# Keys turned by VectorE in blocks of 32 and by transfers through memory, and projected ahead of the queries

## The reference, cut to what matters

```python
# x: 2 sequences of 2048 tokens of 256; H = 16 heads, S = 64, LV = 12 levels
Q, K = x @ Wq.T, x @ Wk.T                     # per head 64 wide
V = x @ Wv.T                                  # per head 16 wide
Lam = softplus(Lp * (x @ Wdl.T))              # 12 level weights per head and token
g = -exp(A_log) * softplus(x @ Wdt.T + dt_bias)
cg = cumsum(g)
scores[t, s] = Q[t] . K[s] / 8
Wmat = scores * exp(cg[t] - cg[s]) * Lam[t, level(t, s)]   # s <= t; level = bit length of s XOR t
o = (Wmat @ V) @ Wout.T + x                   # then layernorm with gain and bias
x = layernorm(x + o)
# then a gated recurrent cell over the 2 sequences (3 gates, 256 wide), outputs through tanh,
# added to x, and a last layernorm
```

## Time and profile before

| | us |
|---|---|
| median of 3 runs | 671.96 |
| lowest, highest | 671.46, 676.09 |
| profiled execution | 675.62 |
| its span | 674.0 |

### The profile page before, as it was taken

The page is one execution under the profiler, slowest core; times in us unless marked ns, Lnnn a source line. Parts: engine busy times, 40 slices in busy tenths (PEclk is TensorE's granted clock), DMA queues, the critical chain, the costliest instruction groups (busy, mean ns, idle before and its releaser), DMA issues.

```text
span 674.0 us, 22147 instructions
## 1 busy us (share of the span) xinstructions
PE 656.2 (97%) x9114; PEld 594.3 (88%) x9114; DVE 486.4 (72%) x1100; ACT 336.9 (50%) x755; POOL 354.1 (53%) x475
## 2 busy tenths in 40 slices
PE   9989999999999999999999999999998999999994
PEld 7889999999999999899999999999987788888894
DVE  3864887779787978676887879787986656655556
ACT  5555454444545454555454445545552343555555
POOL 1806555646464646556554636474883335343425
PEclk9999999999999999999999999999997999999998
DMA  9123130414131222203140313122336403140002
GB/s 304 51 58 64 45 89 28 92 31 88 41 77 54 66 65 67 69 27 87 31 93 28 89 30 88 36 67 74 92 81 126 68 9 62 52 82 31 33 33 93
DMA packets 91987, 45.47 MB, mean 67 GB/s; under 512 B 39664, under 2 KB 90480, under 8 KB 91888
## 3 DMA queue, kind: packets, MB, share of 16 engines
q1 hardware_dynamic: 91888, 44.06, 26.6%
HBM read 34.60 MB, written 9.44 MB: 65 GB/s over the span
## 4 chain that ended last, share of the span: by engine, by line
PE 85%; DVE 6%; ACT 2%; POOL 2%; issue 2%; SPq 1%; DMA 0%; DVEq 0%; POOLq 0%
PE bank L436 64%; PE bank L460 5%; PE bank L439 4%; PE bank L527 4%; PE bank L492 4%; PE bank L556 4%; DVE t L1027 1%; ACT t L790 1%; SPq L347 1%; DVE t L1030 1%; ACT E L790 1%; SPq L370 1%; POOL t L1414 1%; DMA yT<-xscr 0%; POOL yL L1414 0%
## 5 line engine op out<-in xcount | busy, mean ns | idle before, releaser
L436 PE MATMUL bank<-xH,wH 128*128 128x256 f32 x480 | 144.4, 301 | 1.2 <-ACT KT L790 0.9
L436 PE MATMUL bank<-xL,wH 128*128 128x256 f32 x480 | 135.0, 281 | 0.0
L436 PE MATMUL bank<-xH,wL 128*128 128x256 f32 x480 | 134.5, 280 | 0.0
L1027 DVE TENSOR_TENSOR W<-bank,E 128x512 f32<-128x512 f32 x128 | 82.1, 685 | 23.9 <-PE bank L436 23.6
L436 PEld LDWEIGHTS bank<-xH,wH 128*128 128x128 f32 x480 | 90.4, 188 | 7.8 <-issue 7.3
L436 PEld LDWEIGHTS bank<-xL,wH 128*128 128x128 f32 x480 | 90.5, 189 | 0.4
L436 PEld LDWEIGHTS bank<-xH,wL 128*128 128x128 f32 x480 | 90.5, 188 | 0.0
L790 ACT ACTIVATE E<-bank 128x512 f32<-128x512 f32 x128 | 66.1, 602 | 46.8 <-PE bank L460 46.8
L790 ACT ACTIVATE QT<-bank 128x512 f32<-128x512 f32 x64 | 38.2, 597 | 98.5 <-PE bank L436 98.5
L436 PE MATMUL bank<-QT,KT 64*128 64x128 f32 x1024 | 66.3, 280 | 0.0
L436 PEld LDWEIGHTS bank<-QT,KT 64*128 64x128 f32 x1024 | 60.2, 189 | 4.8 <-issue 0.8
(11 more groups left out here) (151 smaller groups left out, 1650.5 us busy)
## 6 DMA issues: line engine op xcount, KB each, us to landing
cB<-scr SPq DMA_DIRECT2D x240, 64.0 KB, 3.0
xt<-in_xT SPq DMA_DIRECT2D x16, 256.0 KB, 2.8
xs<-in_x SPq DMA_DIRECT2D x16, 256.0 KB, 3.2
xscr<-tx SPq DMA_DIRECT2D x32, 128.0 KB, 2.8
yT<-xscr SPq DMA_DIRECT2D x64, 64.0 KB, 2.5
out<-xs SPq DMA_DIRECT2D x16, 256.0 KB, 2.1
xt<-in_wffn SPq DMA_DIRECT2D x8, 256.0 KB, 3.0
QT<-in_wqk SPq DMA_DIRECT2D x4, 256.0 KB, 5.8
```

Source lines behind the costliest of these rows:

```text
L436: return e.matmul(o, a, b, start=start, stop=stop)
L1027: return e.tensor_tensor(o, a, b, op)
```

## The change

TensorE's transposes of keys and ScalarE's copies of them are gone. VectorE turns each quarter of a pair's KT (128x512) in blocks of 32x32 into a buffer kx (`turn_keys`; for pair 0 into W), and SyncE stores it in memory, kscr (`store_keys`). `load_keys` reads a chunk's keys back into Kt with four transfers that put the blocks in their places, in runs of 32 numbers. The state matmuls wait for these. In a pair from the second on, jobs 0, 1, 4, 5 now make K and jobs 2, 3, 6, 7 make Q (`part`). `load_coefs` is split, so that key transfers stand between its parts. x1 is gone (the sum is written in place in xs), tx is one buffer instead of two, and the columns of the second part's weights are ordered to follow the new order of jobs.

```diff
--- before.py
+++ after.py
-SPLIT = [0, 4, 1, 5, 2, 6, 3, 7]
+SPLIT = [4, 5, 0, 1, 6, 7, 2, 3]
...
+def part(sg, j):
+
+    if sg == 0:
+        return j % 2 == 0, j - j % 2
+
+    return j % 4 >= 2, 4 * (j // 4) + 2 * (j % 2)
+
+
+def copied(sg, q):
+
+    return next(j for j in range(8) if part(sg, j) == (False, 2 * q)) + 1
+
+
+def key_jobs(s):
+
+    out = []
+    for d, q in ((7, 0), (5, 1), (3, 2), (2, 3)):
+        if (s + d) % 8 == 0 and 1 <= (s + d) // 8 < NSG:
+            out.append(((s + d) // 8, q))
+    return out
...
-        if s % 4 == 0 and cc < CB - 1:
-            out += [("keys", ci, 0), ("keys", ci, 1)]
...
+        kscr = nc.dram_tensor("kscr", (4 * NSG, 32, 2048), F32, kind="Internal").ap()
...
-        x1 = sb("x1", [P, 256])
-        tx = [sb(f"tx{i}", [P, 256]) for i in range(2)]
+        tx = sb("tx", [P, 256])
+        kx = sb("kx", [P, 512])
...
+            def store_keys(sg, q):
+
+                e.wait_ge(d_kx, 4 * sg + q + 1)
+                src, done = (kx[:, :], l_kx) if sg else (W[:, 4 * q:4 * q + 4, :].rearrange("p h t -> p (h t)"), l_k0)
+                e.dma_start(kscr[4 * sg:4 * sg + 4, :, 512 * q:512 * q + 512].rearrange("i t c -> (i t) c"),
+                            src).then_inc(done, 16)
+
+            def load_keys(ci):
+
+                sg, c = ci // 2, ci % 2
+                e.wait_ge(l_kx, 64 * sg) if sg else e.wait_ge(l_k0, 64)
+                if STATE[ci]:
+                    e.wait_ge(p_st, STATE[ci])
+                for j in range(4):
+                    b = 128 * c + 32 * j
+                    e.dma_start(Kt[32 * j:32 * j + 32, :].rearrange("t (q i f) -> t q i f", q=8, i=4),
+                                kscr[4 * sg:4 * sg + 4, :, :].rearrange("i t (q b) -> t q i b", q=8)[:, :, :, b:b + 32]
+                                ).then_inc(l_Kt, 16)
...
                 for sg, j in token_jobs(s):
                     if j == 5:
-                        load_coefs(sg)
-                        if sg + 2 < NSG:
-                            load_x(sg + 2)
+                        store_coefs(sg)
...
-                if s in (NG - 8, NG - 7):
-                    load_turned(0, s - NG + 8)
                 if (ci := chunk_at(s, 11)) is not None:
                     store_turned(ci)
+                for q in range(4) if s == -2 else ():
+                    store_keys(0, q)
+                for sg, q in key_jobs(s):
+                    store_keys(sg, q)
+
+                if 0 <= s < NG and s % 8 == 3 and s // 4 + 1 in STATE:
+                    load_keys(s // 4 + 1)
+                if -1 <= s < NG - 8 and s % 8 == 7:
+                    load_keys((s + 1) // 4)
+                if s == -1:
+                    load_coefs(0, 1)
+                    e.wait_ge(g_xl, 1)
+                    load_xt(3)
+                    load_x(2)
+                if s in (NG - 10, NG - 7):
+                    load_turned(0, (s - NG + 10) // 3)
+                for sg, j in token_jobs(s):
+                    if j == 5:
+                        load_coefs(sg, 0)
+                for sg, j in token_jobs(s - 1):
+                    if j == 5:
+                        load_coefs(sg, 1)
+                        if sg + 2 < NSG:
+                            load_x(sg + 2)
...
-                    for q in range(4):
-                        t = tr(MB[m][:, 128 * q:128 * q + 128], KT[b][:, 4 * n + q, 128 * c:128 * c + 128])
-                    t.then_inc(p_kt, 1)
...
+                e.wait_ge(l_Kt, 64 * (STATE[ci] + 1))
...
-                b, Q, q = sg % 2, banks[project_bank(j)], j % 2 == 0
-                m0 = j if q else 8 + j - 1
+                b, Q = sg % 2, banks[project_bank(j)]
+                q, m0 = part(sg, j)
+                m0 = m0 if q else 8 + m0
...
-                    act(Kt[:, 512 * n:512 * n + 512], MB[m][:, :], ACT.Copy).then_inc(m_free[m], 1)
...
+                if ci == 0:
+                    e.wait_ge(l_k0, 64)
...
-                e.transpose(tx[ci % 2][:, :], xs[:, ci, :]).then_inc(d_tx, 1)
+                if ci:
+                    e.wait_ge(l_tx, 16 * ci)
+                e.transpose(tx[:, :], xs[:, ci, :]).then_inc(d_tx, 1)
+
+            def turn_keys(sg, q):
+                e.wait_ge(a_qk, 8 * sg + copied(sg, q))
+                src = KT[sg % 2][:, 2 * q:2 * q + 2, :].rearrange("p m t -> p (m t)")
+                if sg == 0:
+                    o = W[:, 4 * q:4 * q + 4, :].rearrange("p h t -> p (h t)")
+                else:
+                    o = kx[:, :]
+                    if sg > 1 or q:
+                        e.wait_ge(l_kx, 16 * (4 * (sg - 1) + q))
+                e.transpose(o, src).then_inc(d_kx, 1)
...
+                if s == -2:
+
+                    for q in range(4):
+                        turn_keys(0, q)
...
+                for sg, q in key_jobs(s):
+                    turn_keys(sg, q)
...
-                    tt(x1[:, :], oo[:, :], xs[:, ci, :], ALU.add).then_inc(g_x1, 1)
+                    tt(xs[:, ci, :], oo[:, :], xs[:, ci, :], ALU.add).then_inc(g_x1, 1)
```

More of the change, by code:

```diff
@@ L29 @@
 B_END = 1200
-WF, WI, WC, UF, UI, UC, WO, UO = range(8)
+GX, GU, WO, UO = (4, 5, 0), (1, 6, 7), 2, 3
 def bc(ap, axis, n):
@@ L337, in load_coefs @@
                 e.dma_start(scr.rearrange("a l c t -> (a l) (c t)"), cT[:, :]).then_inc(l_sc, 16)
+            def load_coefs(sg, c):
                 e.wait_ge(l_sc, 16 * sg + 16)
[L339 to L348, removed]
+                ci = 2 * sg + c
+                if ci in INTER:
+                    if ci >= 2 and ci - 2 in INTER:
+                        for h in range(2):
+                            m, u = MISC["inter", ci - 2, h]
+                            e.wait_ge(m_free[m], u + 1)
+                    for a in range(8):
+                        e.dma_start(cB[c][16 * a:16 * a + 16, :, :, :].rearrange("p l u t -> p (l u) t"),
+                                    scr[a, :, c, :].partition_broadcast(16)).then_inc(l_cB[c], 16)
@@ L355, in load_turned @@
             def load_turned(blk, t):
                 c0 = 16 * t + 4 * blk
-                for i in range(2):
-                    e.wait_ge(l_tx[i], 16 * (c0 // 2 + 2))
+                e.wait_ge(l_tx, 16 * (c0 + 4))
                 if blk == 0:
@@ L391, in _ @@
             load_xt(2)
-            load_coefs(0)
-            e.wait_ge(g_xl, 1)
-            load_xt(3)
-            load_x(2)
+            store_coefs(0)
             for s in STEPS:
-                for i in [i for i in range(8) if s == (NG - 20 if i < 2 else NG - 17 + i)]:
+                for i in [i for i in range(8) if s == (NG - 20 if i < 2 else min(NG - 17 + i, NG - 10))]:
                     load_wf(i)
@@ L592, in first_project @@
             def first_project(j):
-                q = j % 2 == 0
-                Q, m0 = banks[5 * (j % 2)], j if q else 8 + j - 1
+                q, m0 = part(0, j)
+                Q, m0 = banks[5 * (j % 2)], m0 if q else 8 + m0
                 if j < 4:
@@ L646, in first_bias @@
                 e.wait_ge(a_qk, 8 * NSG)
-                e.wait_ge(g_wf, SPLIT.index(UC) + 1)
+                e.wait_ge(g_wf, max(SPLIT.index(w) for w in GU) + 1)
                 e.wait_ge(g_c0, 1)
@@ L751, in _ @@
                 if 0 <= ci < NC:
-                    if n == 0 and ci in STATE:
-                        keys(ci)
                     if n == 1:
@@ L806, in project @@
                 n = 5 * (j % 2) if sg == 0 else project_bank(j)
-                b, q = sg % 2, j % 2 == 0
-                m0 = j if q else 8 + j - 1
+                b = sg % 2
+                q, m0 = part(sg, j)
                 src = banks[n][:, :].rearrange("p (m t) -> p m t", m=2)
@@ L815, in project @@
                     e.wait_ge(p_sc, 4 * (sg - 2) + 4)
+                    e.wait_ge(d_kx, 4 * (sg - 2) + 4)
                 if q:
@@ L989, in _ @@
                     act(c0H[:, :, :], bc(c0, 2, 2), ACT.Copy).then_inc(a_c0, 1)
-                if 0 <= s < NG and s % 4 == 0 and s // 4 in STATE:
-                    keys(s // 4)
                 for sg, j in project_jobs(s):
```

56 lines of the change are left out of this document (18 added, 38 removed).

## The result

The changed kernel takes **724.44 us** (median of 4 runs, 716.97 to 727.8) against 672.10 for the kernel before in the same comparison (4 runs): ratio **1.073**, 95% interval 1.062 to 1.083. It is slower, by about 52 us, where 12 less were forecast, and it lies outside the range. The profiled execution took 727.8 us, its span is 726.0. It is the slowest of the four, and the ratio rests on the other three (716.97 to 726.99).

The account below looks back on a forecast made before the run. TensorE was taken as the bound; -25.5 (transposes) + 11.2 (Kt waits) + 1 (start) + 1 (last pair) = -12.3 us, giving 660 us against a median of 671.96; range 647 to 690 us.

Parts of the forecast that it names:

- What bounds the kernel: TensorE: busy 97% of the span, 85% of the chain of waits; an instruction removed mid-program gives its issue time back.
- The transposes, -25.5: Thirty chunks lose eight key transposes each on TensorE, at a step of 0.85 us per chunk: 25.5 us saved.
- estimate of 94 us: The skill's 390 ns per TensorE turn for 240 transposes, time about 570 us; set aside for the measured 106 ns.
- The Kt wait, +11.2: State matmuls of each pair's first chunk wait 0.8 us for Kt (bounds 0 and 2.7), 14 times: +11.2 us (0 to +38).
- Kt late: Rival: queue ahead of Kt load stretches, landing 6.2 us, wait 2.8 us per pair, about 689 us; chance of late 0.27.
- break-even of 1.7 us: The Kt wait per pair, 23.5 / 14, beyond which the change turns to a loss; over 1% at 2.2 us.
- The clock: TensorE's granted clock might drop to 0.50 behind each new wait: about 1.5 us each, 20 in all, outside the sum.
- VectorE, costed at nothing: Added turns fit VectorE's idle gaps at no cost; rival: turns and store waits pass on 10.5 us, 670 us; shared chance 0.15.
- Kt in time: Rival: Kt loads land in under 4.5 us, only a 0.2 us CT wait shows: -20.7, 651 us; chance 0.20.
- Start: Program start: first Kt lands at 44.6, where the first state would stand at 44.0: +1 us (0 to 3).
- Last pair: Chunk 30's Kt lands at 518.0, state stood at 512.85; mostly offset by the vanishing 2.62 us yL wait: +1 (0 to 6).
- The 19-fold loss: Skill's warning that a DMA copy turning by access pattern is 19 times slower than hardware transpose; judged not to apply here.

Follow-up runs that it names:

- experiment 12: Changed kernel with second cB set and xs load behind Kt loads, two kx buffers, nearly all turns cut to 32 of 512 columns: 667.41 us, ratio 0.990.
- experiment 10: Changed kernel halved: VectorE turns only odd chunks' keys, even ones transposed on TensorE; both turns moved, one behind the state update: 662.41 us, ratio 0.983.
- experiment 7: Changed kernel with second cB set and xs load behind Kt loads, one kx buffer, nearly all turns cut to 32 of 512 columns: 669.34 us, ratio 0.993.
- experiment 1: Changed kernel with a pair's second set of cB loads and its xs load moved behind the first chunk's Kt loads: 680.31 us, ratio 1.009.
- experiment 3: Changed kernel plus 20 useless matmuls before the Kt wait of even chunks 2 to 26: 707.42 us, ratio 1.050.
- experiment 4: Changed kernel with TensorE's key transposes and ScalarE's copies put back; turns, stores and loads stay, no state waits for Kt: 686.14 us, ratio 1.019.
- 5: Changed kernel with second cB set and xs load behind Kt loads, plus a second buffer for turned keys (pairs 1 to 12): 673.48 us, ratio 1.000.
- experiment 2: Changed kernel with Kt loads of the same bytes in 4096-byte runs per partition instead of 128-byte pieces: 686.26 us, ratio 1.020.
- experiment 9: Changed kernel, two kx buffers, second cB set behind Kt, first yT loads behind last Kt, turns moved to idle places, pair 14's cB behind weights: 674.30 us.
- 6: Changed kernel with second cB set and xs load behind Kt loads, two kx buffers, first eight yT loads behind the last Kt load: 674.05 us, ratio 1.000.

## Why the prediction was wrong

**What bounds the kernel**: right. TensorE is busy over 91% of the interior in every row above, and what the experiments took out of its waits and its slow clock came back in the time.

**The transposes, -25.5**: right in kind, too large. One row pair gave a step of 0.85 us; the interior of experiment 12 gives 0.70 (17.6 / 25), so 30 chunks are worth 21.1; by experiment 10 (busy TensorE 9.4 us less for 12 chunks) it is 0.78, or 23.5. In experiment 7 the first matmul comes 1.02 us behind the start of the weighing (340.60 to 341.62), as the first transpose did before (314.70 to 315.71), so there the whole 0.85 is saved. Yet a whole chunk took 13.76 us (338.46 to 352.22) against 14.38 before, only 0.62 less: elsewhere in the chunk some is lost again, 0.12 of it in the ng piece, which starts 0.98 us behind wo,yt instead of 0.86. One step was taken where a whole period should have been. The prediction's estimate of 94 us for the transposes was carried to "about 570 us"; with the other terms of the sum it gives 592, without them 578. Nothing else rests on it.

**The Kt wait, +11.2: this step failed.** Its parts: issue of the first Kt load 10.4 us after the store of keys 2, measured 11.0 in the pair above, near enough. From that issue to the state 5.3 us were taken, between bounds of 4.1 and 7.2. Measured are 6.1 to 8.3, 7.1 in the mean over the 14 pairs. The 5.3 took the *transfer* time of the yT set and left out what the *issue* takes: a Kt load of 1024 pieces holds the queue 0.98 us (3.9 for four, mean), a cB or yT load 0.53 to 0.59. Three such issues and the landing, 4.1 us in experiment 1 (the page's median, against yT's 2.5), are 7.0. I had put aside the upper bound, which was the very same number of pieces, timed in full. With 7.1 the wait is 2.6 us by the prediction's own sum; 2.4 was measured. In the list of rivals this was "Kt late", and its break-even of 1.7 us was passed. By itself it adds 22 us to the forecast, 14 waits of 2.4 us instead of 0.8, and turns the gain of 12 into a loss of 10.

**The clock, left out of the sum.** It stood in the rival as 1.5 us a wait, 20 us. It belonged to every case with a wait. In the interior TensorE was busy 413.8 us; with the same instructions at full clock in experiment 12, 391.0. So **22.8 us** of the loss is slow clock (18.8 if experiment 1, with its small waits, is the measure), 1.75 us for each of the 13 Kt waits of the interior, near the 1.5 that the rival had. The granted clock of the interior, 0.95 in its row, gives some 23 us without any comparison, and experiment 3 won 17 us back by doing more work.

**VectorE, costed at nothing**: wrong, but hidden in the changed kernel, since the waits for Kt gave VectorE time to catch up. It shows when they are gone: experiment 4 puts the price of the added work at 12.3 us with nothing gained, most of it waits for VectorE, 5 puts the store wait out of kx at 8.0 us of TensorE (named as a rival, with 3.2 us of landing against 3.65 of work before the next turn; but the store sits behind loads in the queue, and the wait for it was up to 2.6 us). The first rival, "Kt in time", with its 651 us, was therefore too good: with Kt in time the kernel takes 680, with the second buffer 673.

**The ends**. Start: +1 forecast, 2.2 measured, inside its bounds, but by luck. The first state was to wait for the late Kt; it stood at 47.23, 2.4 us later than before, with no wait in front of it, though its Kt was issued at 37.50. What came instead was a longer wait for ng, a result of VectorE, and the low clock right behind it (0.57 over 42 to 46 us). Before the change the same matmul stood at 40.38, with 0.53 us of wait; now:

```profile
41.46 0.63 PE L495 MATMUL bank<-ng,cs 128*128 128x32 f32 x4 [1.51 <-DVE ng L1061]
```

Then chunk 2 waited 1.26 us for its Kt, about what the missing transposes of two chunks had given. Last pair: +1 (0 to 6) forecast, 7.5 measured, with a Kt wait of 5.8 us. The 6.0 of wait had been computed, and setting it off against yL's wait was right: that wait of 2.62 us is gone from the list. What was left out is a wait for CT, 2.5 us where 1.0 stood before, one of 0.6 for KT, and the clock. From the state of chunk 28 to the end TensorE is idle 5.1 us longer than before (18.4 against 13.3) and busy 2.4 us longer, at a mean granted clock of 0.92 against 0.96 (columns as in the rows of the interior; before, then after):

```profile
484.92:674.00 189.08, 175.74 (x1599) 153.14 (x1598) 116.23 (x254) 92.92 (x182) 86.32 (x120) 0.96 0.27 63
```

```profile
529.40:726.00 196.60, 178.18 (x1582) 155.18 (x1582) 120.16 (x257) 91.84 (x179) 86.46 (x120) 0.92 0.32 70
```

**The 19-fold loss** by which the Trainium skill (VectorE: DVE Perf Modes, "The three transpose paths") warns of strided copies does not show: Kt lands in a median of 4.1 us (experiment 1) where yT took 2.5, and in long pieces in 3.1 (experiment 2). No run has the hardware transpose that the page compares with.

**The sum, mended**: in the interior -17.6 for the transposes, +37.1 idle (31.9 of it the 13 Kt waits) and +22.8 clock, which is the 42.3 measured (the clock's share is worked out from the other two, so that it must fit; the clock row's 23 us is the check on it); with 2.2 and 7.5 for the ends it is the 52.0 between the spans.

What stays open: which of the moved turns in experiment 9 makes yt late; how much of the price of the added work in experiment 4 is the turns, and how much the transfers and the order of projections; and what the 3 to 6 us at the ends of experiments 1, 5, 6, 7, 9 and 12 consist of beyond the waits named.

## What to carry to other kernels

Where a term is "issue plus landing", time the whole set of the nearest transfer with the same number of pieces from first issue to first use, and take that; a figure made of halves of it is a guess. A new wait of some 1.5 us or more on a busy TensorE is to be priced twice, as idle time and as slow clock behind it. When an engine at 70 to 80% gets more work, do not ask only how much slack it has, but what stands right behind each place: with half of the turns, and the one in front of the state update put behind it, the kernel gained 1.7% (0.4% of that from the order of the last transfers); with all of them, in the two placings tried, nothing.

## What the runs showed of the hardware

Issuing a DMA on SyncE takes longer with more pieces: 0.33 to 0.47 us for most stores of 256 KB and loads of xs, 0.50 to 0.62 for a cB load, 0.72 to 1.3 for 1024 pieces of 128 bytes (means over a set of four; single ones took 0.56 to 2.4, with a median of 0.71), and 0.45 for the same 128 KB in long pieces (experiment 2, median 0.42). The queue is held meanwhile, so everything behind pays. The Trainium skill (Perfetto Trace Analysis, "DMA Optimizations") advises to spread issues over several engines where the issuing is the limit; that was not tried here.

In the changed kernel the granted clock fell to the 1.2 GHz level at the end of, or within 1.7 us after, each idle time of TensorE of 1.5 to 4.0 us in the interior, and stayed there for some microseconds while TensorE worked; the two Kt waits of 1.26 and 1.28 us were not followed by a fall. The length of a wait alone does not decide it: in experiment 2 a wait of 1.40 us was followed by a fall, and waits of 1.87 and 2.15 us were not. Useless matmuls in the idle time kept the clock up (0.977 against 0.943 in the mean).
